# The second normalization of an attention and feed-forward kernel in another order, and the hidden row clipped by GpSimd and rounded by ScalarE

## What is computed

```python
def bit_linear(x, w, b):
    gamma_x = clip(max(abs(x), axis=-1), 1e-5)
    scale_x = 127.0 / gamma_x
    x_dq = clip(round(x * scale_x), -128, 127) / scale_x
    gamma_w = clip(mean(abs(w)), 1e-5)
    w_dq = clip(round(w / gamma_w), -1, 1) * gamma_w
    return x_dq @ w_dq.T + b

x = x + attention(layernorm(x), context)
y = layernorm(x)                       # the second normalization
gate, val = silu(bit_linear(y, gate_w, gate_b)), bit_linear(y, val_w, val_b)
x = x + bit_linear(gate * val, out_w, out_b)
```

## Time and profile before

| | |
|---|---|
| time before, median of 3 runs | 970.87 us (970.19 to 971.57) |
| the profiled execution's own time | 969.66 us |
| its span, first to last instruction | 967.6 us |
| PE busy | 876.3 us (91%) |
| DVE busy | 834.3 us (86%) |
| ACT busy | 528.2 us (55%) |
| POOL busy | 556.3 us (57%) |
| granted TensorE clock, mean | 0.954 |

### The profile page before, as it was taken

How to read it: one execution, slowest core, us unless ns; L and a number is a source line. 1 busy time by engine, 2 the same in 40 slices (tenths; PEclk the granted TensorE clock), 3 DMA queues, 4 the chain that set the end, 5 groups by cost and what they waited for, 6 DMA issues and landing times. The chain is left out here.

```text
span 967.6 us, 15479 instructions
## 1 busy us (share of the span) xinstructions
PE 876.3 (91%) x4290; PEld 672.3 (69%) x4290; DVE 834.3 (86%) x1234; ACT 528.2 (55%) x885; POOL 556.3 (57%) x551
## 2 busy tenths in 40 slices
PE   3556999999999999999999999999999798738996
PEld 2434888878888788878888888888888676313543
DVE  6756899988998999899989988998899778686996
ACT  2315556655655575566656655665566477443332
POOL 5176646465555746574657465646464678664661
PEclk9768999999999999999999999999999998778999
DMA  8000121011101110111011101110210168100000
GB/s 302 0 21 27 55 67 36 27 40 47 46 14 50 46 35 24 39 46 35 24 39 46 35 24 44 50 39 20 66 46 14 34 252 306 52 0 12 22 22 33
DMA packets 25174, 51.73 MB, mean 53 GB/s; under 512 B 5440, under 2 KB 11840, under 8 KB 23872
## 3 DMA queue, kind: packets, MB, share of 16 engines
q1 hardware_dynamic: 24064, 49.36, 15.8%
q10 hardware_dynamic: 1088, 2.10, 0.6%
HBM read 49.35 MB, written 2.10 MB: 53 GB/s over the span
## 5 line engine op out<-in xcount | busy, mean ns | idle before, releaser
L791 POOL TENSOR_TENSOR rot_cos<-rot_cos,rot_sin 128x512 f32<-128x512 f32 x93 | 120.1, 1291 | 147.3 <-DVE rot_sin L985 135.7
L895 ACT ACTIVATE probs<-scores,neg_max 128x1024 f32<-128x1024 f32 x128 | 144.0, 1126 | 74.8 <-DVE neg_max L1011 74.0
L976 DVE TENSOR_TENSOR pt_lo<-banks,pt_hi 128x512 fp32r<-128x512 f32 x256 | 164.3, 683 | 9.8 <-ACT pt_hi L879 7.5
L879 ACT CAST pt_hi<-banks 128x512 fp32r<-128x512 f32 x256 | 138.3, 596 | 54.5 <-PE banks L1154 54.5
L1011 DVE TENSOR_REDUCE neg_max<-scores 128x1 f32<-128x1024 f32 x128 | 155.8, 1218 | 9.9 <-PE scores L1171 9.0
L1154 PE MATMUL banks<-ident,probs 128*128 128x128 f32 x1024 | 134.8, 275 | 10.0 <-PEq L1213 5.4
L1154 PEld LDWEIGHTS banks<-ident,probs 128*128 128x128 f32 x1024 | 119.9, 141 | 28.7 <-issue 5.8
L799 POOL TENSOR_TENSOR rot_lo<-rot_cos,rot_hi 128x512 fp32r<-128x512 f32 x93 | 119.7, 1287 | 7.8
L1006 DVE SCALAR_TENSOR_TENSOR acc<-banks,inv,acc 128x512 f32<-128x512 f32 x128 | 92.6, 747 | 12.9 <-PE banks L1086 10.9
L1086 PE MATMUL banks<-pt_hi,v_hi 128*128 128x512 f32 x256 | 102.9, 402 | 0.9
L1086 PE MATMUL banks<-pt_hi,v_lo 128*128 128x512 f32 x256 | 101.0, 394 | 0.0
(11 more groups left out here) (194 smaller groups left out, 2014.4 us busy)
## 6 DMA issues: line engine op xcount, KB each, us to landing
load<-in_pack SPq DMA_DIRECT2D x15, 320.0 KB, 2.9
raw_chunk<-in_out_w SPq DMA_DIRECT2D x8, 512.0 KB, 3.7
load<-in_pack SPq DMA_DIRECT2D x16, 256.0 KB, 2.7
raw_chunk<-in_gate_w SPq DMA_DIRECT2D x8, 512.0 KB, 3.6
raw_chunk<-in_val_w SPq DMA_DIRECT2D x8, 512.0 KB, 4.3
raw<-in_gate_w SPq DMA_DIRECT2D x4, 1024.0 KB, 5.8
raw<-in_val_w SPq DMA_DIRECT2D x4, 1024.0 KB, 5.1
raw<-in_out_w SPq DMA_DIRECT2D x4, 1024.0 KB, 5.2
```

Source lines behind the costliest of these rows:

```text
L791: nc.gpsimd.tensor_tensor(total, total, rot_sin[:, c, :], ALU.add).then_inc(rot_sum, 1)
L879: nc.scalar.copy(out, src).then_inc(group_hi, 1)
L895: nc.scalar.activation(probs[:, u % 2, :], scores[:, u % 2, :], ACT.Exp, bias=neg_max[:, u:u + 1], accum_out=sums[:, u:u + 1]).then_inc(ex ...
L976: return nc.vector.tensor_tensor(pair[1], src, pair[0].bitcast(F32), ALU.subtract)
```

## The change

The second normalization: VectorE takes only `bn_stats` of a tile. `deviation` makes the inverse deviation and the shift right after the root; ScalarE normalizes into four buffers (one for each tile of a half); VectorE takes the maximum of the absolute values of each normalized tile (`extreme`), and when it has four, `scales` makes the quantization scale. GpSimd multiplies by it and adds MAGIC, and in a second operation clips on both sides. TensorE transposes, into the PSUM room of the scores, and ScalarE, no longer VectorE, takes the tile out (`take`).

The hidden row: GpSimd clips (`clip`, behind the third of its four products), ScalarE rounds (`round_down`, behind the fourth silu), VectorE's copy has no maximum left. The turn of row h-2 stands after projection 3 instead of 1 and the contraction after projection 6 instead of 4, on TensorE and on VectorE alike. Rows 0 to 3 are written out and rows 4 to 7 are two turns of the loop. The last row's path (`last_range` and what follows) keeps its order.

```diff
 LAST_ACT:
-    ("drop", 6), ("T", 7, 1), ("drop", 7), ("drop", 8), ("V", 1), ("root", 0), ("drop", 9), ("norm", 0), ("norm", 1),
-    ("norm", 2), ("norm", 3),
+    ("drop", 6), ("T", 7, 1), ("drop", 7), ("root", 0), ("norm", 0), ("norm", 1), ("V", 1), ("norm", 2), ("norm", 3),
+    ("drop", 8), ("drop", 9), ("take", 0), ("take", 1), ("take", 2), ("take", 3),
 LAST_DVE:
-    ("O", 0, 2), ("O", 0, 3), ("T", 5, 1), ("stats", 2), ("T", 6, 0), ("T", 6, 1), ("T", 7, 0), ("stats", 3),
-    ("T", 7, 1), ("stats", 0), ("stats", 1), ("spread", 0), ("V", 1), ("scale", 0), ("O", 1, 0), ("O", 1, 1),
-    ("O", 1, 2), ("O", 1, 3), ("X", 0), ("X", 1), ("X", 2), ("X", 3),
+    ("O", 0, 2), ("O", 0, 3), ("T", 5, 1), ("stats", 0), ("stats", 1), ("T", 6, 0), ("T", 6, 1), ("T", 7, 0),
+    ("stats", 2), ("T", 7, 1), ("stats", 3), ("spread", 0), ("deviation", 0), ("extreme", 0), ("extreme", 1), ("V", 1),
+    ("extreme", 2), ("extreme", 3), ("scale", 0), ("O", 1, 0), ("O", 1, 1), ("O", 1, 2), ("O", 1, 3),
+TOKENS_LIFTED = {(2, 0): 4, (2, 2): 5, (3, 0): 6, (3, 2): 7}
+TOKENS_TURNED = {(2, 7): 4, (3, 2): 5, (3, 5): 6, (3, 7): 7}
+TOKENS_TAKEN = {(3, 0): 4, (3, 1): 5, (3, 2): 6, (3, 3): 7}
 SecondNorm:
     def statistics(self, dve, u):
         nc.vector.bn_stats(self.stats[:, u, :], tile)
-        nc.vector.tensor_reduce(self.most[:, one], tile, AX, ALU.max)
-        nc.vector.tensor_reduce(self.least[:, one], tile, AX, ALU.min).then_inc(self.seen, 1)
+    def deviation(self, dve, b):
+        inverse_deviation(nc, dve, self.var_eps[:, half], self.root[:, half], rstd, self.tmp[:, half], self.root_ready, b + 1,
+                          lambda ins: self.link(dve, ins))
+        nc.vector.scalar_tensor_tensor(out=self.shift[:, half], in0=self.mv[:, half, 0], scalar=-1.0, in1=rstd, op0=ALU.mult,
+                                       op1=ALU.mult).then_inc(self.shift_ready, 1)
+    def extreme(self, dve, u):
+        dve.wait_ge(self.normed_ready, u + 1)
+        self.nc.vector.tensor_reduce(self.most[:, u:u + 1], self.tile(u), AX, ALU.max,
+                                     apply_absolute_value=True).then_inc(self.most_ready, 1)
     def lift(self, pool, u):
-        pool.wait_ge(self.normed_ready, u + 1)
-        self.nc.gpsimd.tensor_scalar(self.lifted[:, u % 2, :], self.normed[:, u % 2, :], MAGIC, MAGIC + 127, ALU.add,
-                                     ALU.min).then_inc(self.lifted_ready, 1)
+        pool.wait_ge(self.scale_ready, u // U + 1)
+        self.nc.gpsimd.tensor_scalar(tile, tile, self.x_scale[:, u:u + 1], MAGIC, ALU.mult, ALU.add).then_inc(self.lifted, 1)
+        pool.wait_ge(self.lifted, u + 1)
+        self.nc.gpsimd.tensor_scalar(tile, tile, MAGIC + 127, MAGIC - 128, ALU.min, ALU.max).then_inc(self.clipped, 1)
+    def take(self, act, u, src):
+        act.wait_ge(self.turned, u + 1)
+        self.nc.scalar.activation(self.t["xt"][:, :, u * P:(u + 1) * P], src.rearrange("p (c s) -> p c s", c=KD),
+                                  ACT.Identity, bias=self.t["minus_magic"][:]).then_inc(self.taken, 1)
 ffn, TensorE:
+                if n == 0:
+                    pe.wait_ge(second.taken, h.number + 1 if h.i is None else NU)
-                    if before == 2 and n == 1:
+                    if before == 2 and n == 3:
                         turn(h.plus(-2))
-                    if before == 2 and n == 4:
+                    if before == 2 and n == 6:
                         contract(h.plus(-2))
+                    if h.i is None and (h.number, n) in TOKENS_TURNED:
+                        turn_tokens(TOKENS_TURNED[h.number, n])
 ffn, VectorE:
                     scale(h, n, before)
-                    if before == 2 and n == 1:
+                    if before == 2 and n == 3:
                         copy_ht(h.plus(-2))
                     if before and n == 2:
                         range_of(h.plus(-1))
-                    if before == 2 and n == 4:
+                    if before == 2 and n == 6:
                         finish(h.plus(-2))
-                    if before and n == 5:
-                        round_down(h.plus(-1))
+                    if before == 1 and n == 3:
+                        second.deviation(dve, 1)
+                    if before == 1 and n >= NP - 2:
+                        second.extreme(dve, 2 * (n - NP + 2) + U)
+                        second.extreme(dve, 2 * (n - NP + 2) + U + 1)
+                    if h.i is None and h.number == 2 and n == 0:
                         second.scales(dve, 1)
 ffn, ScalarE:
+            def round_down(h):
+                act.wait_ge(h_clipped, h.after(1, 1))
+                if not (h.i is None and h.number == 0):
+                    act.wait_ge(ht_full, h.after(1, 0))
+                nc.scalar.activation(h_quant[:], hidden[:, h.number % 2, :], ACT.Identity,
+                                     bias=t["minus_magic"][:]).then_inc(h_rounded, 1)
                     silu(h, n, before)
                     if before and n == 1:
                         lift(h.plus(-1))
+                    if before == 1 and n:
+                        second.normalize(act, U + n - 1)
+                    if h.i is None and (h.number, n) in TOKENS_TAKEN:
+                        second.take(act, TOKENS_TAKEN[h.number, n], ps_x[:])
+                    if before and n == NH - 1:
+                        round_down(h.plus(-1))
+                    if before == 1 and n == NH - 1:
+                        second.normalize(act, NU - 1)
 ffn, GpSimd:
+            def clip(h):
+                pool.wait_ge(h_lifted, h.after(1, 1))
+                nc.gpsimd.tensor_scalar(tile, tile, MAGIC + 127, MAGIC - 128, ALU.min, ALU.max).then_inc(h_clipped, 1)
+                    if before and n == 2:
+                        clip(h.plus(-1))
+                    if h.i is None and (h.number, n) in TOKENS_LIFTED:
+                        second.lift(pool, TOKENS_LIFTED[h.number, n])
```

More of the change, by code:

```diff
@@ L66 @@
 A0, A1, V1, V0, C0, C1 = ("A", 0, "next"), ("A", 1, "next"), ("V", 1, "last"), ("V", 0), ("C", 0, "next"), ("C", 1, "next")
-UNGROUPED = ("score", "max", "exp", "sum", "double", "abs", "drop", "stats", "spread", "root", "scale", "norm")
+UNGROUPED = ("score", "max", "exp", "sum", "double", "abs", "drop", "stats", "spread", "root", "deviation", "norm", "extreme", "scale", "X", "take")
 PE_ORDER = (
@@ L534, in link, with spread @@
         dve.wait_ge(self.chain, self.links)
+    def spread(self, dve, b):
+        nc, half = self.nc, slice(b * U, (b + 1) * U)
+        dve.wait_ge(self.seen, U * (b + 1))
+        for u in range(b * U, (b + 1) * U):
+            ins = nc.vector.bn_aggr(self.mv[:, u, :], self.stats[:, u, :])
+        self.link(dve, ins)
+        nc.vector.tensor_scalar(self.var_eps[:, half], self.mv[:, half, 1], EPS, None, ALU.add).then_inc(self.var_ready, 1)
     def deviation_root(self, act, b):
@@ L564, in scales @@
-        link(nc.vector.tensor_scalar(x_gamma, tmp, 1e-5, 1.0 / 127.0, ALU.max, ALU.mult))
-        link(nc.vector.reciprocal(self.x_scale[:, half], x_gamma))
-        link(nc.vector.tensor_tensor(factor, rstd, self.x_scale[:, half], ALU.mult))
-        nc.vector.scalar_tensor_tensor(out=self.shift[:, half], in0=mean, scalar=-1.0, in1=factor, op0=ALU.mult,
-                                       op1=ALU.mult).then_inc(self.scale_ready, 1)
+        x_gamma = t["x_gamma"][:, half]
+        dve.wait_ge(self.most_ready, U * (b + 1))
@@ L569, in scales @@
+        self.link(dve, nc.vector.tensor_scalar(x_gamma, self.most[:, half], 1e-5, 1.0 / 127.0, ALU.max, ALU.mult))
+        nc.vector.reciprocal(self.x_scale[:, half], x_gamma).then_inc(self.scale_ready, 1)
         for w, name in enumerate(("x_gate", "x_val")):
             nc.vector.tensor_scalar(t[name][:, half], x_gamma, t["gamma"][:, w:w + 1], None, ALU.mult)
-    def normalize(self, act, u):
-        act.wait_ge(self.scale_ready, u // U + 1)
-        if u >= 2:
-            act.wait_ge(self.lifted_ready, u - 1)
-        self.nc.scalar.activation(self.normed[:, u % 2, :], self.t["acc"][:, u, :], ACT.Identity, bias=self.shift[:, u:u + 1],
-                                  scale=self.factor[:, u:u + 1]).then_inc(self.normed_ready, 1)
@@ L933, in period @@
                         second.normalize(act, item[1])
+                    elif item[0] == "take":
+                        second.take(act, item[1], turned_tokens(item[1]))
                     else:
@@ L1069, in period @@
                         second.spread(dve, item[1])
+                    elif item[0] == "deviation":
+                        second.deviation(dve, item[1])
+                    elif item[0] == "extreme":
+                        second.extreme(dve, item[1])
                     elif item[0] == "scale":
@@ L1146, in products @@
                     mm = three(out, [x[:, j * P:(j + 1) * P] for x in cv], [x[:] for x in m])
-                elif kind == "X":
-                    mm = second.turn(pe, group[1], out)
                 else:
```

(17 more changed lines are left out.)

98 lines of the change are left out of this document (29 added, 69 removed).

## The result

| | before | changed kernel |
|---|---|---|
| time, median | 970.74 us (970.19 to 971.57, 5 runs) | 964.29 us (959.96 to 965.97, 5 runs) |
| ratio | | 0.9921, interval [0.9893, 0.9949] |
| profiled execution, span | 969.66, 967.6 us | 965.97, 964.2 us |
| the same kernels, first batch of experiments | 968.97 (965.44 to 973.74, 17 runs) | 963.01 (961.19 to 966.01, 6 runs), 0.9939 [0.9916, 0.9963] |

So the medians differ by 6.5 us, and by 6.0 in the first batch of experiments, where I had said 2.3 us (968.6). The direction was right, the size was not; the time lies at the lower edge of the range.

A forecast was written before the change was run, and what follows sets the result against it. The prediction took TensorE to bound the loop (busy 45.23 of 45.30 us), with time to be had in the stretch before it. Terms -1.4, -7.0, +4.7 and +1.5 gave -2.2 us, forecast 968.6 us, range 964.0 to 973.0.

The forecast's parts named there:

- The end of the last head: Up to the feed-forward stage's start: fewer VectorE reductions and shorter GpSimd lifts, -1.4 us, bounds -3.2 and -1.2.
- Rows 0 to 3: First four feed-forward rows: 60.5 us from the stage's start instead of 67.5, -7.0 us, bounds -4.6 and -10.4.
- the walk of row 0: First feed-forward row: eight reductions gone, scales end about 3.5 us earlier, row 1's first scale at 847.6.
- The prediction's own sign of failure: Rows 1 to 3: forecast fails if the granted clock differs much from 0.75, or GpSimd's 512-column operations from 0.62 us.
- the 128x1 operations: VectorE's small operations in row 1: assumed to wait for GpSimd, 2.2 us, bound 0.
- rival (2): Rows 4 to 7: late rounding makes small operations meet GpSimd's product, up to 1.27 us more a row, 973.7; chance 0.14.
- Rows 4 to 7: Loop rows: a cycle of waits through maximum, copy and contraction makes rows 12.4 us instead of 11.25, +4.7 us.
- (3): Rows 4 to 7: the cycle of waits does not close, rows of 11.25 us, 964.0; chance 0.05.
- (4): GpSimd's 512-column operations cost 1.9 instead of 0.62 us: +10 in the head, +3.6 later, 982; chance 0.04.
- Behind the last projection: After the last projection: row 6's turn 2.0 us late behind ScalarE's rounding, +1.5 us, bounds +0.3 and +3.
- the page figure of the Trainium skill: GpSimd's clip: 4.5 us for a 2048-column two-input add; so priced, the estimate would be 11 us slower.
- Rival (1): Head and first four rows: mild GpSimd waits, clock kept, -3.2 and -10.4, 963.5, or half of both, 966; chance 0.20.

The follow-up runs named there:

- fill_before: Kernel before plus six unread identity transposes behind each of the four token tiles' transposes in the last head; 965.37 us, ratio 0.9975.
- reclip2_fill: reclip2 plus 14 unread identity transposes behind the transposes of token tiles 0, 1 and 2; 969.73 us, ratio 1.0006.
- reclip2: Changed kernel with GpSimd clipping each of the last head's four token tiles three times instead of once; 971.15 us, ratio 1.0014.
- con7: Changed kernel with the contraction of row h-2 and VectorE's finish moved behind projection 7 instead of 6; 959.72 us, ratio 0.99.
- row_only: Kernel before with only the new hidden row (GpSimd clips, ScalarE rounds, later turn and contraction), old normalization; 977.75 us, ratio 1.0095.
- norm_pw: Changed kernel with the old hidden row, GpSimd's tenth weight lot waiting for the shift, V's cast ahead of the norms; 952.77 us, ratio 0.9821.
- norm_tail4: norm_tail plus nine unread matmuls before the transposes of token tile 7 in row 3; 948.73 us, ratio 0.9779.
- norm_pool: Changed kernel with the old hidden row and GpSimd's tenth weight lot waiting for the shift, V's cast unmoved; 951.31 us, ratio 0.981.
- norm_tail: norm_pool plus 16 unread matmuls behind the last projection; 949.83 us, ratio 0.9789.
- late_turn: Changed kernel with TensorE transposing the last head's four token tiles only after GpSimd clipped the last one; 964.53 us, ratio 0.996.

## Why the prediction was right or wrong

**The end of the last head: right.** With the 2.03 us of the exponential added, my walk is met link by link: statistics end at 817.54 (I had 815.4, so 817.4), shift at 824.98 (825.2), TensorE's attention matmuls at 827.91 (828.1), the last clip at 835.52 (835.4), the stage at 837.48 (837.1). The gain is 1.1 us, and 0.2 to 1.1 in the five profiles that have this head as it is (26.32 to 27.24 us): a little less than my bounds. A lift and a clip of 512 columns take 0.71 and 0.61 us where I had 0.62 for both.

**Rows 0 to 3: the step that failed.** Measured from the stage's start, changed kernel against my walk:

| | walk | measured | |
|---|---|---|---|
| row 1's first scale | 12.5 | 9.97 | -2.5 |
| deviation done | 22.1 | 18.4 | -3.7 |
| tile 7 normalized | 29.6 | 25.8 | -3.8 |
| contraction of row 0 starts | 37.4 | 33.6 | -3.8 |
| row 4 starts | 60.5 | 56.35 | -4.15 |

The step that failed is the walk of row 0: "its scales end about 3.5 us earlier after the start", and row 1's first scale "comes at 847.6", 12.5 us behind the start. It came at 9.97, and the scales of row 0 ended 8.18 us behind the start against 13.65 before, 5.5 earlier. Behind the sentence stood a pace that I did not write down, that of the earlier trace rows, 11.85 us for 40 matmuls, as if it belonged to the matmuls. Its start was at the low clock, and that level changed with what TensorE does ahead of the stage: in fill_before and reclip2_fill the fillers there came with a high start. reclip2 and reclip2_fill price it at 2.1. The prediction's own sign of failure said so: it wanted a granted clock near 0.75 over rows 1 to 3, and the changed kernel has 0.90 (844.40 to 893.83). The next 1.1 is the 128x1 operations, which I let wait for GpSimd. They don't. The timelines of DVE and then POOL in the changed kernel:

```profile
851.73 0.15 DVE L1475 TENSOR_SCALAR h_gamma<-h_max 128x1 f32<-128x1 f32 x1
851.92 0.21 DVE L1477 TENSOR_SCALAR h_out<-h_gamma,gamma 128x1 f32<-128x1 f32 x1
...
852.97 1.06 DVE L293 TENSOR_TENSOR tmp_second<-rstd_second 128x4 f32<-128x4 f32 x1
854.07 1.18 DVE L294 TENSOR_TENSOR tmp_second<-tmp_second,var_eps_second 128x4 f32<-128x4 f32 x1
```
```profile
851.52 1.26 POOL L1606 TENSOR_TENSOR acc<-acc,out_bias 128x512 f32<-128x512 f32 x1
852.74 2.49 POOL L1627 TENSOR_TENSOR hidden<-sigma,val 128x512 f32<-128x512 f32 x2
```

Two tensor_scalars of 128x1 ran 0.15 and 0.21 us in the middle of GpSimd's 851.52 to 852.78; the two-input ones of 128x4 waited 0.9 and 1.0, as did 128x4 tensor_scalars elsewhere (L295 above). The rule of the Trainium skill that rival (2) cited ("SBUF — State Buffer", section "Who interferes with whom") agrees with all of these that waited. For a tensor_scalar the section says only that it can contend, when its operands meet the conditions of a two-port mode; I passed over that condition when I wrote that by the rule the 128x1 ones would wait too. Apart from these two sizes the order of the waits was as walked: tile 7 is normalized behind the rounding, for which VectorE idles 3.08 us, the contraction waits 3.24 us and is partly low (5.28 us, I had 5.8), row 4 waits for the take of tile 7. Of the 4.15 us the clock has 2.1, the small operations 1.1; of the rest 0.4 lies ahead of row 1's first scale and 0.35 behind the start of that contraction, and its cause was not traced.

**Rows 4 to 7: right.** Period 12.41 (12.4), wait before the contraction 0.98 to 1.27 (1.2), +4.9 us (+4.7). con7 and row_only show the mechanism. Rivals (2), (3) and (4) did not come: the small operations behind the maximum take 0.15 to 0.21 us each, the rows are not 11.25, and GpSimd's 512-column operations take 0.61 to 0.71.

**Behind the last projection: right.** +1.8 (+1.5); the turn waits 2.27 us for ScalarE's rounding (2.0).

**The rivals' prices.** GpSimd's clip took 1.89 us for 2048 columns, so the page figure of the Trainium skill ("GPSIMD Engine Reference", "Performance versus the Vector engine") doesn't bear on it. Rival (1) has the time nearest to the measured one, 963.5, but that is mostly luck: the head gave 1.1 us and not its 3.2, and the contraction where it let the clock be kept was partly low (5.28 us). Of its terms only the 128x1 operations came true; the clock was kept in row 0, where I had not looked. (The chances of my list make 0.30 for the same and 0.20 for slower, not 0.29 and 0.21.)

## What to carry to other kernels

A change that rebuilds what lies ahead of a stage can change the clock in which the stage begins: never carry a pace at the low level over from the old trace without saying what kept TensorE idle there. When an operation moves off a busy engine, draw the ring through the new order first; here VectorE was freed of 1.22 us a row, and by the order that went with it the row became 1.16 us longer, so that half of the change was worth more than the whole. Where a chain of small VectorE operations meets a long GpSimd operation whose result nobody needs soon, a semaphore can pay: holding one lot of weights back by 0.9 us gave 2.4 to 2.9.

## What the runs showed of the hardware

- The attention's last exponential began anywhere from 807.04 to 811.16 us in 17 profiled executions, and 17 runs of the kernel before on one chip lay between 965.44 and 973.74, where the first three had lain within 1.4 us. To place a difference of a few us, stretches of the profile measured from a common event were needed here.
- Row 0's level is not set by the program alone: in two profiles of the new normalization (norm_pw, norm_tail4) it was low, 0.427 us a matmul, for 8 matmuls. norm_tail4 has the head of norm_pool and norm_tail, whose profiles were high, and TensorE idled only 0.83, 0.83 and 1.03 us ahead of it; late_turn with 2.17 and 1.46 was high. What decides it stays open.
- A 128x1 tensor_scalar on VectorE ran beside a GpSimd operation in 0.15 us; a 128x4 one waited up to 1.7 us for its end.
